# An attention stage on one core: row sums turned over as 64x64 and spread through memory, norm scaling moved to GpSimd

## What is computed

```python
x = x + 0.5 * ffn(layernorm(x))
x = x + attn(layernorm(x))
x = x + 0.5 * ffn(layernorm(x))

def attn(x):                                  # b=8, s=512, d=256, 16 heads of 16
    q, k, v = proj(W_q), proj(W_k), proj(W_v)
    scores = q @ k.T / sqrt(16);  scores = where(causal, scores, -65504)
    out = softmax(scores) @ v
    return out @ W_o.T
```

## Time and profile before

| | |
|---|---|
| time, median of 3 runs | 1724.15 us (1717.61 to 1724.71) |
| the profiled execution's own time | 1726.3 us |
| its span from first to last instruction | 1724.6 us |
| mean granted TensorE clock | 0.952 of full |
| busy: PE, DVE, ACT, POOL | 1565.3, 956.8, 582.7, 522.2 us |
| attention, from its first matmul to the last chunk's logits | 624.6 to 1168.4 us |

### The profile page before, as it was taken

One profiled execution on the slowest core, in us unless ns is written; L12 is line 12 of the kernel. 1 busy time (PEld: TensorE's weight loads), 2 busy tenths in 40 slices (PEclk: granted clock), 3 DMA queues, 4 the chain that ended last, 5 costly groups with the idle time before them and its releaser, 6 DMA issues. The chain is left out here.

```text
span 1724.6 us, 27588 instructions
## 1 busy us (share of the span) xinstructions
PE 1565.3 (91%) x8355; PEld 1146.8 (66%) x8389; DVE 956.8 (55%) x1908; ACT 582.7 (34%) x1110; POOL 522.2 (30%) x768
## 2 busy tenths in 40 slices
PE   6699999999999949899998998866999899999998
PEld 5688885666668836566665665535888666666787
DVE  5377643333336646777778676634775333333466
ACT  1332222222223215555555554424222222222232
POOL 3328802333320022233233232212387033333200
PEclk9999999999999968899999999967999999999999
DMA  7678732222237243333443343225196322222561
GB/s 232 217 259 295 275 113 86 86 85 86 88 129 257 75 124 89 88 109 103 119 114 99 106 115 101 67 77 173 51 343 220 104 83 85 89 88 85 182 221 50
DMA packets 174904, 231.36 MB, mean 134 GB/s; under 512 B 18114, under 2 KB 134338, under 8 KB 174802
## 3 DMA queue, kind: packets, MB, share of 16 engines
q1 hardware_dynamic: 155698, 173.42, 32.9%
q0 software_dynamic: 19104, 56.64, 9.3%
HBM read 113.27 MB, written 82.84 MB: 114 GB/s over the span
## 5 line engine op out<-in xcount | busy, mean ns | idle before, releaser
L943 PE MATMUL f_bank<-f_xparts,f_sw 128*128 128x512 f32 x1536 | 382.3, 398 | 23.8 <-DVE f_sw L881 19.9
L943 PEld LDWEIGHTS f_bank<-f_xparts,f_sw 128*128 128x128 f32 x1536 | 285.6, 192 | 81.6 <-issue 26.0
L1007 PE MATMUL f_bank<-f_ew,f_hid 128*128 x640 | 305.6, 600 | 3.4 <-ACT f_hid L654 3.4
L1516 DVE TENSOR_REDUCE at_mx<-at_ps 128x1 f32<-128x384 f32 (+3 forms) x352 | 213.3, 634 | 134.2 <-PE at_ps L1651 126.8
L612 POOL DMA_INDIRECT outputs_by_choice<-f_xq,f_home x160 | 153.1, 957 | 428.9 <-DVE f_xq L904 406.1
L1425 ACT ACTIVATE at_pT<-at_ps 128x512 f32<-128x512 f32 (+1 forms) x352 | 194.0, 559 | 124.2 <-PE at_ps L1667 113.9
L1371 POOL TENSOR_SCALAR_AFFINE_SELECT at_pT<-at_pT 128x128 f32<-128x128 f32 (+2 forms) x352 | 130.6, 376 | 310.3 <-ACT at_pT L1425 306.1
L894 DVE COPY f_hid<-f_bank 128x256 f32<-128x256 f32 x160 | 67.9, 425 | 245.0 <-PE f_bank L1015 245.0
L1647 PE MATMUL at_ps<-at_kT,at_qT 96*128 96x512 f32 (+2 forms) x384 | 155.5, 422 | 47.7 <-DVE at_mx L1516 41.3
L647 ACT ACTIVATE f_sil<-f_bank 128x256 f32<-128x256 f32 x160 | 61.3, 383 | 355.1 <-PE f_bank L1007 355.1
L1007 PEld LDWEIGHTS f_bank<-f_ew,f_hid 128*128 128x128 f32 x640 | 114.8, 190 | 98.6 <-issue 90.1
(11 more groups left out here) (159 smaller groups left out, 1926.6 us busy)
## 6 DMA issues: line engine op xcount, KB each, us to landing
f_ew<-in_L_ffn_routed_w_dram SPq DMA_DIRECT2D x96, 256.0 KB
f_rawx<-rows_by_slot SPq DMA_DIRECT2D x160, 128.0 KB, 1.9
f_ew<-outputs_by_choice SPq DMA_DIRECT2D x16, 1024.0 KB, 7.6
rows_by_slot<-zero POOLq DMA_DIRECT2D x10, 1024.0 KB, 18.4
f_rawx<-xn_turned SPq DMA_DIRECT2D x16, 512.0 KB
f_xq<-xn_rows POOLq DMA_DIRECT2D x32, 256.0 KB
at_qT<-at_hiT SPq DMA_DIRECT2D x64, 128.0 KB, 2.8
at_kT<-at_hiT SPq DMA_DIRECT2D x128, 64.0 KB, 2.6
```

Source lines behind the costliest of these rows:

```text
L943: ins = pe.matmul(ps[j % 2][:, :], sw12[:, wp, k, w, j * P:(j + 1) * P], xparts[:, u, xp, k, :], start=(i == 0), stop=(i == 3 * KD - 1))
L1007: ins = pe.matmul(rUp[r % 2][:, :], xsT[:, r % 2, k * P:(k + 1) * P], w12[:, bass.ds(e * (KD * 2 * RH) + k * 2 * RH, 2 * RH)], start=(k == ...
L1516: v.tensor_reduce(own, ps1[i % RING1][:, 0:heads * w].rearrange("p (j a x) -> p j a x", a=min(heads, 2), x=w), AX.X, ALU.max).then_inc(mx_ ...
```

## The change

1. `take_out` no longer copies all 64 odd rows of `oT` to `sums`. It takes one row per head (4 rows of 512) and lays them as 32 partitions x 64. A half is then 64 partitions x 64.
2. `scale` is split. `turn_over` (step 1) takes the reciprocal of that 64x64 tile. `send` (step 2, SP) writes it to memory, `fetch` (step 4, SP, ahead of `lay_out`) waits for that and reads it back, each head's row repeated for its 16 partitions, into `rec` 128x512. The product stands at step 7.
3. `project_out` goes from step 7 of gr = 1 and 2 to step 9 of gr = 1 and step 5 of gr = 2; `route` goes from step 2 to step 5 of gr = 0.
4. All 64 tiles of `normalize` go to POOL, one in a step: behind attention at gr = 3, steps 1 to 4, ahead of it at gr = 3, steps 6 to 9.
5. The statistics go in two halves: gr = 3, steps 3 and 4 (were all at 5), and gr = 2, steps 8 and 9 (were all at 9).
6. `turn_max`, `shift` and `lay_max` go from step 1 to step 2.

```diff
-    AT_MAX, AT_PROJ, AT_WEIGH, AT_SCALE, AT_OUT = 1, 4, 8, 3, 7
+    AT_MAX, AT_PROJ, AT_WEIGH = 2, 4, 8
+    AT_TURN, AT_SEND, AT_FETCH, AT_SCALE, AT_OUT = 1, 2, 4, 7, {1: 9, 2: 5}
...
-        return ours(i // NG - 2, 0, NB_) if i % NG == 0 and s == 2 else None
+        return ours(i // NG - 2, 0, NB_) if i % NG == 0 and s == 5 else None
...
-        sums = m.sb("sums", [P, KD, CHUNK])
+        sums = m.sb("sums", [H // KD * 8, KD, CHUNK // 8])
+        turned = m.sb("turned", [H // KD * 8, KD, CHUNK // 8])
...
-                for dst, lo in ((av, 0), (sums, 1)):
-                    sp.dma_start(dst[at:at + HD, gr // 2, :], oT[lo:P:2, G % 2, :]).then_inc(o_ld[G % 2], 16)
+                sp.dma_start(av[at:at + HD, gr // 2, :], oT[0:P:2, G % 2, :]).then_inc(o_ld[G % 2], 16)
+                sp.dma_start(sums[to:to + HG * 8, gr // 2, :], oT[1:P:2 * DK, G % 2, :]).then_inc(o_ld[G % 2], 16)
+
+            def send(c, k):
+                sp.wait_ge(rc, 2 * c + k + 1)
...
+                sp.dma_start(dram.rec[k].rearrange("h (x n) -> (h x) n", x=8), turned[:, k, :]).then_inc(rec_out, 16)
+
+            def fetch(c, k):
+                sp.wait_ge(rec_out, 16 * (2 * c + k + 1))
...
+                sp.dma_start(rec[:],
+                             dram.rec[k].rearrange("h (o n) -> h o n", o=1).to_broadcast([H // KD, DK, CHUNK])
+                             ).then_inc(rec_in, 16)
...
+            def normalize(i, t, dst, src):
+                return p.tensor_scalar(dst[:, t, :], src[:, t, :], mv[:, i, t, 0:1], rstd[:, i, t:t + 1],
+                                       ALU.subtract, ALU.mult)
...
-            def scale(c, k):
+            def turn_over(c, k):
...
-                v.reciprocal(rec[:], sums[:, k, :]).then_inc(rc, 1)
-                dve.wait_ge(rc, 2 * c + k + 1)
+                v.reciprocal(turned[:, k, :], sums[:, k, :]).then_inc(rc, 1)
+
+            def scale(c, k):
+                dve.wait_ge(rec_in, 16 * (2 * c + k + 1))
                 v.tensor_tensor(attnT[:, k, :], av[:, k, :], rec[:], ALU.mult).then_inc(scaled, 1)
...
-                    if gr == 3 and s == 5 and 1 <= c + 2 < NB_:
-                        moments1(c + 2)
+                    if gr == 3 and s in (3, 4) and 1 <= c + 2 < NB_:
+                        moments1(c + 2, s - 3)
```

More of the change, by code:

```diff
@@ L1138, in out_of @@
         c = ours(i // NG - 1, 0, NB_)
-        return (c, i % NG - 1) if i % NG in (1, 2) and s == AT_OUT and c is not None else None
+        return (c, i % NG - 1) if AT_OUT.get(i % NG) == s and c is not None else None
     def turn2_of(i, s):
@@ L1145, in route_of, with half_of @@
     def route_of(i, s):
-        return ours(i // NG - 2, 0, NB_) if i % NG == 0 and s == 2 else None
+        return ours(i // NG - 2, 0, NB_) if i % NG == 0 and s == 5 else None
+    def half_of(i):
+        c = ours(i // NG if i % NG == 3 else i // NG - 1, 0, NB_)
+        return (c, i % NG % 3) if i % NG in (1, 3) and c is not None else None
     AUX = {}
@@ L1226, in attention @@
         rc = m.sem("rc")
+        rec_out = m.sem("rec_out")
+        rec_in = m.sem("rec_in")
         scaled = m.sem("scaled")
@@ L1338, in _ @@
                         sp.dma_start(dram.xnT[:, :, bass.ds((c - 2) * CHUNK, CHUNK)], xnT2[:]).then_inc(xnT2_st, 16)
+                    if s == AT_SEND and half_of(i) is not None:
+                        send(*half_of(i))
+                    if s == AT_FETCH and half_of(i) is not None:
+                        fetch(*half_of(i))
                     if s == AT_PROJ and proj_of(i, s) is not None:
@@ L1390, in _ @@
             deviation(0, 0, var1, eps1, rs1)
+            for t in range(CT):
+                normalize1(0, t)
             done(p.memset(identb[:], 0.0))
@@ L1490, in _, with moments @@
             v = nc.vector
-            def moments(i, src, count, var):
-                for t in range(CT):
+            def moments(i, src, part, count, var):
+                for t in range(part * CT // 2, (part + 1) * CT // 2):
                     v.bn_stats(stat[:, i, t, :], src[:, t, :]).then_inc(st, 1)
+                if part == 0:
+                    return
                 dve.wait_ge(st, count + CT)
@@ L1500, in moments @@
                 ins.then_inc(var, 1)
[L1502 to L1505, removed]
-                ins.then_inc(done, 1)
             def maxima(G, n):
@@ L1567, in _, with moments1, moments2 @@
             stats = [0]
-            def moments1(c):
+            def moments1(c, part):
                 dve.wait_ge(x1_ld[c % 2], 16 * (c // 2 + 1))
-                moments(0, x1[:, c % 2], stats[0], var1)
-                stats[0] += CT
-            def normalize1(c):
-                dve.wait_ge(rs1, c + 1)
-                normalize(0, xn, x1[:, c % 2], normed1)
-            moments1(0)
+                moments(0, x1[:, c % 2], part, stats[0], var1)
+                stats[0] += CT * part
+            def moments2(c, part):
+                for u in range(2):
+                    dve.wait_ge(*gone("out", (c, u)))
+                moments(1, xres, part, stats[0], var2)
+                stats[0] += CT * part
+            for part in range(2):
+                moments1(0, part)
             v.memset(mx[:], 0.0).then_inc(mx_clear, 1)
-            normalize1(0)
             dve.wait_ge(w_hi, 4 * KD + 1)
```

61 lines of the change are left out of this document (38 added, 23 removed).

## The result

The changed kernel took 1708.58 us (median of 6 runs, 1703.83 to 1709.93), against 1719.38 us for the kernel before on the same chip. The ratio is 0.9922, 95% interval 0.9901 to 0.9944: faster by 0.8%, where 3.4% was forecast. The prediction had the sign right and the size wrong, and its range, 1655 to 1692, does not hold the time. The profiled execution took 1703.97 us. All ratios here compare executions in the chip's usual state only; the one execution outside it, of the changed kernel in experiment 9, took 1997.01 us at a mean granted clock of 0.745 and is left out.

A forecast was written before the change was run, and what follows sets the result against it. Attention was taken as bound by PE plus stalls behind long DVE pieces. Gains of 67.6 us (40 + 22.9 + 4.7) less costs of 4.9 + 3.5 + 0.3 gave -58.9 from 1724.15: 1665 us, range 1655 to 1692.

The forecast's parts named there:

- the POOL tile: Norm tiles moved to POOL: 0.55 us each, eight adding 4.4 us a chunk to POOL, hidden in the steady part.
- rival C: Round gr = 3: POOL's tile of p us is long, POOL needs 6.2 + 8p; about 1760 us; chance 0.04.
- DVE's product held up by POOL: In `scale`: POOL work may shut out DVE's product, at most 14 x 0.55 = 7.7 us, giving 1673.
- the fetch: Reciprocals' trip through memory: send 2.0 plus fetch 2.9 us, product at step 7 1 to 2 us late, hidden.
- rival A: Step 7: send 3.4 and fetch 4.1 us, so the product blocks DVE until PE's banks run out; 1692; chance 0.12.
- signs of being wrong: In the profile after: clock still low at gr = 3, `at_rec` wait over 3 us, or POOL's tile over 1 us.
- Half clock: Steps 7 and 8 of gr = 3, after the stall: 3.27 us lost in each of seven chunks, 22.9 us to gain.
- no such sequel: Round gr = 1: its 1.91 us stall is not followed by half clock, as its round shows a clock of 1.00.
- Start and end: Outside the steady part: start +0.3 us for POOL tiles; end +3.5 us for send, fetch and tiles less the shorter reciprocal.
- the maxima's rows: Step 6, first reader of the turned maxima: PE waits 0.35 us in two rounds of four, 4.9 us over seven chunks.
- The maxima a step later: `turn_max` a step later, with the statistics in halves: the 4.7 us of PE's waits there go.
- rival D: Stalls only move: the reciprocal is short but PE waits elsewhere as long; time within 0.5%; chance 0.03.

The follow-up runs named there:

- experiment 9: Also called after_again: the changed kernel itself, unedited, run again on the chip of the last experiments; 1699.27 us, ratio 0.9903 to the kernel before.
- all_scale: Changed kernel with all norm tiles on DVE, the product at step 10 and `project_out` at gr = 2, steps 4 and 6; 1665.42 us, ratio 0.9706.
- as_max1: all_scale with the turn of the maxima put back from step 2 to step 1; 1657.28 us, ratio 0.9664.
- turn2_late: Changed kernel with `turn2` of gr = 3 at steps 9 and 10, not 7 and 10; 1698.6 us, ratio 0.9893.
- norm2_dve: Changed kernel with the four norm tiles behind attention back on DVE, one a step; 1677.22 us, ratio 0.9793.
- experiment 10: Also called norm2_scale: changed kernel with the edits of norm2_dve and scale_late together, the norm ahead of attention left on POOL; 1660.89 us, ratio 0.9678.
- out_late: Changed kernel with `project_out` of both halves moved to gr = 2, steps 4 and 6; 1712.32 us, ratio 0.9963.
- scale_late: Changed kernel with the product at step 10, not 7, and `project_out` at gr = 2, steps 4 and 6; 1687.94 us, ratio 0.9844.
- fetch16: Changed kernel with the reciprocals written to memory twice, so the fetch reads 16 rows for 8 partitions each, not 8 for 16; 1697.38 us, ratio 0.9884.
- x1_late: Changed kernel with the 512 KB load of x moved from step 3 to step 8 of gr = 1; 1698.4 us, ratio 0.9895.

## Why the prediction was wrong

**Right: what bound the kernel.** (Of the "three" rounds that the prediction calls nearly full only two are: gr = 1 is busy for 13.13 of 15.04 us, which its sum then counts as a stall.) PE waited for DVE's maxima because of the 3340 ns reciprocal and the block of norm and statistics. With these gone the waits of the earlier trace rows fell from 46.0 to 1.7 us, 44.3 where 44.7 was forecast, and DVE's busy time in gr = 3 is 10.15 us (9.8 forecast). That most of the forecast gain was there is shown by all_scale, which keeps the small reciprocal and gives the two mis-sized terms room: 0.9706, that is 50 us of the 58.9. That its 1665.4 us look like the forecast 1665 is luck, since the kernel before took 1715.16 on that chip and not 1724.15. as_max1, 0.9664, comes to 58 us.

**Failed: the POOL tile, the main step.** The prediction took 0.55 us from bounds of 0.4 to 2.4, put the cost of the tiles in the steady part at nothing ("Both hidden") and wrote that from 0.9 us a tile the cover is thin. It was 1.22, and the cover was gone: `turn2` waited 2.2 to 2.9 us in each of seven chunks, 16.7 in all. By rival C's formula, 6.2 + 8p, POOL then needs 16.0 us for the round gr = 3, and the round took 16.40. So this is rival C's mechanism in its first half: POOL falls behind in steps 1 to 4 and PE waits for it at step 7. That POOL's total sets the round is not shown: by 875.91 POOL waits for ACT again, and PE's wait with the half clock behind it already makes the 16.40. I chose from the cheap end, near POOL's one-input cut, but a cut of 256 columns is 407 to 484 ns and this tile is 2.5 to 3 times that. The row of 2384 ns for 1024 columns with two inputs was no nearer in kind. From bounds so far apart I should have taken a middle value (1.0 by ratio, 1.4 by difference) and seen that it lay past my own mark of 0.9. turn2_late shows that POOL is late in itself, norm2_dve that taking four tiles away mends it. The other thing that the prediction weighed, DVE's product held up by POOL, did not grow: its mean was 800 ns before, 734 after and 692 in all_scale. By the Trainium skill ("GPSIMD Engine Reference", "Elementwise — side-by-side cycle accounting") the prediction had estimated 0.38 us and dispatch for such a tile; 1.22 was measured, and the measurement decides. With the rule of the same section of the Trainium skill, that elementwise work stays on DVE, this case agrees where POOL has a reader waiting (the tile takes 0.391 us on DVE), and not where it has none (experiment 10).

**Failed: the fetch, the second step.** The sum took 2.0 + 2.9 us for send and fetch, with the product 1 to 2 us late and that hidden. The send landed in 1.7. The fetch took 4.6 to 7.0 us in a round, beyond rival A's 4.1 in all of them, and DVE waited 3.1 to 5.1 for it. This is rival A's late product. Its path to PE was another one, though: A let PE run out of score banks, for 3.7 us a chunk, but the score tiles waited 1.5 us in all, and `project_out` at step 9, which the sum had not looked at, waited 1.7 a chunk. The half clock behind some of these waits comes on top. Rival A's path shows only in out_late, where the score tiles wait 17.7 us. Together with scale_late this tells that what stands behind the product counts, and not the projection alone. Two of the prediction's own signs of being wrong have come, POOL's tile over 1 us and the wait for `at_rec` over 3.

**Half clock.** The 22.9 us were to go. In the trace after, ten rounds of attention still have a granted clock of 0.80 to 0.91. Against like rounds at 1.00 in the same trace they have 18.4 us more of PE's busy time: 11.8 in six rounds gr = 3 (one of them in the first chunk, which has no `turn2` yet), 5.1 in three rounds gr = 1 and 1.6 in one of gr = 0. The last round, from 1094.12, is low too and is not in this count. The prediction's "no such sequel" for the 1.91 us stall was read from one chunk: in the trace before, the first such round (721.54 to 738.03) has 0.90.

**Start and end.** Forecast +0.3 and +3.5; measured +3.0 (four POOL tiles take 5.12 us, four on DVE took 2.13) and +6.1. (By the prediction's own sum for the end, 4 x 0.15, the start should have stood at +0.6; it changes nothing.) Both misses of 2.6 to 2.7 us are the POOL tile again, 4 x 0.67.

**The account.** The stage from the first load to the last logits took 553.4 us and now 534.9; the forecast amounts to 494.5, so 40.4 us are missing. The waits of `turn2` and `project_out` (16.7 + 11.6), the half clock (18.4) and start and end (5.3) make 52.0. Against it the maxima's rows waited 2.2 us and not 4.9, which leaves 9 us of gain that I had not counted. Of these I can place two: the first round of attention, 2.6 us shorter with its clock at 1.00 and not 0.67, and a round gr = 1 of before at 0.90 (1.5 us). The rest stays open. It is near the noise: in the trace of after_again the same stage takes 540.1 us, 5.2 more. The two profiled executions also lie further apart (1726.3 and 1703.97) than the medians (1719.38 and 1708.58), so this is an account of two executions and not of the 10.8 us between the medians.

The two terms are worth 10 us (scale_late, 0.9844 against 0.9903) and 19 us (norm2_dve, 0.9793) singly, and 39 together (norm2_scale, 0.9678); norm2_dve and norm2_scale have about 3.4 us of it from the end, where DVE's tiles are shorter. That together they give more than the sum of both may lie in the clock, which falls behind either wait; the intervals are wide, and this is argued and not shown.

**The maxima a step later.** I gave it 4.7 us. It shows no gain in either setting. In the kernel before, the wait only moves, which is what rival D said of the whole; without the long pieces there is nothing to cover. Since the first reader of the maxima's rows waits in all_scale (4.6 us) and not in as_max1, the edit has a small price.

**What stays open.** The fetch takes 4.6 to 7.0 us in a round and 3.75 at the end (issue at 1122.94, product at 1126.69). The shape of the read is 2.3 us of this at gr = 3 (5.8 to 3.5 on average, fetch16), the rows' load 0.7 at gr = 1 (x1_late). The nine copies of `lay_out` issued right behind it were not moved, but the last rounds of attention have none: there the fetch takes 3.8 and 3.9 us (issues at 1074.14 and 1097.72), also inside a round. So these copies are the likely rest of the 8-row read's time; a run that moves them is missing. So is one with both the new shape and the load moved. Open is also why the clock falls in some rounds and not in like ones (below).

## What to carry to other kernels

Where the bounds of a cost that no row shows are a factor of four or more apart, work out the value at which the cover is gone, and let the chance of passing it decide, not the value that is most convenient: here 0.9 us was written down and the middle of the bounds lay beyond it. An operation may be slow where nobody waits for it within its round (POOL's tiles in steps 6 to 9), but not three to six steps ahead of its reader (steps 1 to 4 for a turn at step 7). A consumer that waits for a DMA on an in-order engine should be put where nothing urgent is queued behind it; moving what depends on it (out_late) only shows the same wait elsewhere.

## What the runs showed of the chip

- The scaling of a 128x256 fp32 tile with two values per partition takes 1215 to 1283 ns on POOL and 391 to 427 on DVE (the kernels after and all_scale), where POOL's cut of as many columns takes 407. The number of columns alone did not tell POOL's price.
- DVE's reciprocal: 538 ns for 64 columns (on 64 partitions) beside 3340 for 512 (on 128). A line through these two points is 6.25 ns a column and 138 ns fixed, an estimate. A straight share (418 ns) left out the fixed part.
- A 256 KB read of eight rows of memory spread over 128 partitions: 3.75 to 3.9 us from issue to use with nothing issued behind it, 4.6 to 7.0 with other copies issued around it. The same bytes read as 16 rows: 3.3 us with nothing behind it, 3.3 to 3.9 with the copies behind it (fetch16). The 16 KB write ahead of it lands in 1.7 us.
- In the changed kernel the granted clock fell to its half level for a part of the round behind the wait of `turn2` (2.2 to 2.9 us) in six of seven rounds gr = 3, and in gr = 1 behind 2.57 and 2.83 us, but not behind 1.13, 1.33 and 1.78. It did behind 1.52 us in the round from 1013.12, where the projection took 3.33 us and not 1.97; the round ahead of that one had 0.89 with PE busy throughout. all_scale, too, has a round (970.04 to 985.42) with PE busy throughout and a clock of 0.89, with only 0.95 us of idle time in the round ahead. So the length of a wait alone does not tell where the clock falls.
